# Deferring an elementwise product and respreading matmuls in a Mamba block kernel on eight NeuronCores

## The reference, cut to what matters

```
xn = layernorm(x)                          # x: 16 x 2048 x 1024
xp = xn @ in_proj_w.T + b ; x1, x2 = split(xp)         # 2048 channels each
u  = silu(causal_conv4(x1))
h[t] = dA * h[t-1] + dB * u[t] ; y = sum_n C[n] h[n]   # 16 states per channel
s  = (y * silu(x2)) @ out_proj_w.T + b
hid = silu(xn @ wg.T / 127) * (xn @ wu.T / 127)        # 3072 hidden
g  = silu(hid @ wd.T / 127)
out = x + s * g
```

## Time and profile before

| what | us |
|---|---|
| median of the two runs | 5023.45 (5015.12 and 5031.77) |
| profiled execution, its own time | 4871.78 |
| its span on the slowest core (core 5) | 4870.2 |
| spans of the eight cores | 4815.3 to 4870.2 |
| PE, DVE, ACT busy on core 5 | 3108.9, 2581.7, 1166.5 |

### The profile page before, as it was taken

How to read it: one execution, slowest core, us unless ns; L and a number is a source line. 1 busy time by engine, 2 the same in 40 slices (tenths; PEclk the granted TensorE clock), 3 DMA queues, 4 the chain that set the end, 5 groups by cost and what they waited for, 6 DMA issues and landing times.

```text
span 4870.2 us, 40584 instructions; the slowest of 8 cores (4815.3 to 4870.2 us)
## 1 busy us (share of the span) xinstructions
PE 3108.9 (64%) x14080; PEld 1331.7 (27%) x14080; DVE 2581.7 (53%) x1507; ACT 1166.5 (24%) x1575; POOL 169.4 (3%) x324
## 2 busy tenths in 40 slices
PE   3565666666656478767646666656666654777787
PEld 2222222222222134333322222222222221333333
DVE  2777777877777501000137877777778783010001
ACT  6111111111111023432351111111111111334322
POOL 0000000000000000000000000000000000000000
PEclk9777777777777599999868777777777776999877
DMA  3000100011000334432320010001000003353222
GB/s 93 18 18 16 26 18 18 16 26 18 18 15 18 84 57 104 85 49 52 88 64 18 18 24 18 18 15 26 18 18 20 18 11 99 55 139 48 46 44 61
DMA packets 84574, 196.07 MB, mean 40 GB/s; under 512 B 10272, under 2 KB 27040, under 8 KB 84384
## 3 DMA queue, kind: packets, MB, share of 16 engines
q0 software_dynamic: 46080, 109.07, 14.0%
q1 hardware_dynamic: 38304, 84.40, 5.1%
HBM read 268.93 MB, written 33.55 MB: 62 GB/s over the span
## 4 chain that ended last, share of the span: by engine, by line
PE 39%; DVE 25%; issue 22%; ACT 11%; DMA 2%; SPq 1%; DVEq 0%; ACTq 0%; POOLq 0%
DVE bfb L593 22%; PE ps_a L444 7%; PE ps_b L444 6%; ACT bfa L162 5%; PE ps_a L807 4%; PE ps_b L499 4%; PE ps_b L807 4%; PE ps_y L613 4%; PE ps_a L499 3%; PE ps_a L709 3%; PE ps_b L709 2%; DVE bfb L601 2%; ACT s_sb L457 1%; ACT bfb L162 1%; PE ps_t L155 1%
## 5 line engine op out<-in xcount | busy, mean ns | idle before, releaser
L593 DVE TENSOR_TENSOR_SCAN bfb<-aa,bfb 128x2048 bf16<-128x2048 f32 x512 | 2262.1, 4418 | 155.0 <-PE ps_y L613 107.1
L613 PE MATMUL ps_y<-bfb 128*128 128x512 bf16 x2048 | 745.6, 504 | 1021.0 <-DVE bfb L601 1021.0
L613 PEld LDWEIGHTS ps_y<-bfb 128*128 128x128 bf16 x2048 | 211.5, 114 | 1495.7 <-issue 1412.3
L467 DVE TENSOR_TENSOR bfa<-s_sb 128x1024 bf16<-128x1024 bf16 x96 | 66.5, 692 | 1017.9 <-ACT s_sb L457 1017.9
L444 PE MATMUL ps_a<-xnt,bfa 128*128 128x512 bf16 x1536 | 418.1, 421 | 288.8 <-ACT bfa L162 285.8
L749 DVE TENSOR_TENSOR bfb<-f32a,s_sb 128x1024 bf16<-128x1024 f32 x32 | 39.2, 1225 | 824.0 <-PE ps_t L155 643.6
L162 ACT ACTIVATE bfa<-ps_t 128x1024 bf16<-128x1024 bf16 x320 | 319.4, 1020 | 255.9 <-PE ps_t L155 251.9
L444 PE MATMUL ps_b<-xnt,bfa 128*128 128x512 bf16 x1536 | 377.0, 390 | 0.0
L499 PE MATMUL ps_a<-xnt,bfa 128*128 128x512 bf16 x1024 | 322.3, 472 | 2.6 <-ACT bfb L520 1.4
L499 PE MATMUL ps_b<-xnt,bfa 128*128 128x512 bf16 x1024 | 317.8, 466 | 0.0
L444 PEld LDWEIGHTS ps_a<-xnt,bfa 128*128 128x128 bf16 x1536 | 146.9, 104 | 484.6 <-issue 376.8
(11 more groups left out here) (60 smaller groups left out, 1835.7 us busy)
## 6 DMA issues: line engine op xcount, KB each, us to landing
f32a<-x SPq DMA_DIRECT2D x64, 512.0 KB, 7.6
bfa<-wg POOLq DMA_DIRECT2D x96, 256.0 KB, 3.6
bfa<-wu POOLq DMA_DIRECT2D x96, 256.0 KB, 3.6
bfb<-wd POOLq DMA_DIRECT2D x32, 768.0 KB, 6.7
bfa<-win POOLq DMA_DIRECT2D x64, 256.0 KB, 5.8
xg_spill<-bfb SPq DMA_DIRECT2D x32, 512.0 KB, 2.6
bfa<-wout POOLq DMA_DIRECT2D x32, 512.0 KB, 5.2
bfb<-xg_spill SPq DMA_DIRECT2D x128, 128.0 KB, 6.4
```

The costliest lines, as they stand in the source:

```text
L467: (lambda mh: lambda e: e.tensor_tensor(bfa[:, 8192 + 1024 * mh:8192 + 1024 * (mh + 1)], s_sb[:, 0:1024], s_sb[:, 1024:2048], ALU.mult))(mh),
L593: (lambda i, n, hs, uslot: lambda e: e.tensor_tensor_scan(hs, sb["aa"][:, 16 * i + n:16 * i + n + 1].broadcast_to([128, T]), uslot, 0.0, A ...
L613: (lambda n, pc, dg, hs: lambda e: e.matmul(ps["y"][:, 512 * pc:512 * (pc + 1)], dg, hs[:, 512 * pc:512 * (pc + 1)], start=(n == 0), stop= ...
```

## The change

The product of both halves is no longer appended right after the unit with hi = 1. It is put on a list and appended to DVE's queue at the start of the next `emit_f1` (`flush_hm`). `s_sb` has two slots for the halves, by mh mod 2, and PE's wait before a unit with hi = 0 is for the product of mh - 2. The units inside a block move from n = 4 and 8 to n = 6 and 12, the convolution from n = 9 to n = 13, and the input pieces 4 and 5 from behind the gate product to n = 9 and 11.

```diff
+        pending_hm = []
+
+        def flush_hm():
+            while pending_hm:
+                mh, sl = pending_hm.pop(0)
+                wh = [("ss", ev_mm_evac[(mh, 1, 1)])] + \
+                    ([h_guard[0]] if mh == 0 else [])
+                ev_hm[mh] = op("vector",
+                               (lambda mh, sl: lambda e: e.tensor_tensor(
+                                   bfa[:, 8192 + 1024 * mh:8192 + 1024 * (mh + 1)],
+                                   s_sb[:, 2048 * sl:2048 * sl + 1024],
+                                   s_sb[:, 2048 * sl + 1024:2048 * sl + 2048],
+                                   ALU.mult))(mh, sl),
+                               waits=wh, inc="sv")
+                ev_hm_prev[0] = ev_hm[mh]
 
         def emit_f1(u, cb, count):
             for _ in range(count):
+                flush_hm()
...
                             if p == 0 and hi == 0:
-                                w.append(("sv", ev_hm_prev[0]))
+                                w.append(("sv", ev_hm[mh - 2] if mh >= 2
+                                          else ev_hm_prev[0]))
...
-                    dst = s_sb[:, 1024 * hi + 512 * p:1024 * hi + 512 * (p + 1)]
+                    dst = s_sb[:, 2048 * sl + 1024 * hi + 512 * p:
+                               2048 * sl + 1024 * hi + 512 * (p + 1)]
                     wev = [("st", lastm)]
-                    if g_guard[0] is not None:
+                    if g_guard[0] is not None and mh <= 1:
                         wev.append(g_guard[0])
-                        g_guard[0] = None
...
                 if hi == 1:
-                    wh = [("ss", ev_mm_evac[(mh, 1, 1)])] + \
-                        ([h_guard[0]] if mh == 0 else [])
-                    ev_hm[mh] = op("vector",
...
+                    pending_hm.append((mh, sl))
...
-                if n in (1, 3, 5, 7) and i + 1 < NI:
+                if n % 2 == 1 and n <= 11 and i + 1 < NI:
                     emit_ip_piece(i + 1, n // 2)
-                if n in (4, 8):
+                if n in (6, 12):
                     emit_f1(u, 0, 1)
-                if n == 9 and i + 1 < NI:
+                if n == 13 and i + 1 < NI:
                     emit_conv(i + 1)
...
             if i + 1 < NI:
-                emit_ip_piece(i + 1, 4)
-                emit_ip_piece(i + 1, 5)
                 emit_ip_piece(i + 1, 6)
                 emit_ip_piece(i + 1, 7)
```

More of the change, by code:

```diff
@@ L425, in emit_f1 @@
                 f1_idx[0] += 1
+                sl = mh % 2
                 wnm, act = (("wg", AF.Silu) if hi == 0 else ("wu", AF.Identity))
@@ L461, in emit_f1 @@
                     rot.release(idx, "ss", ev_mm_evac[(mh, hi, p)])
+                if mh == 1 and hi == 1:
+                    g_guard[0] = None
                 ws_f1.consumed(slot, lastm)
                 if hi == 1:
-                    wh = [("ss", ev_mm_evac[(mh, 1, 1)])] + \
-                        ([h_guard[0]] if mh == 0 else [])
-                    ev_hm[mh] = op("vector",
[L467 to L472, removed]
+                    pending_hm.append((mh, sl))
         ip_state = {}
```

## The result

The changed kernel's median is 4358.87 us (11 runs, 4253.44 to 4475.77), that of the kernel before 4921.65 us (10 runs, 4829.57 to 5031.77). The ratio is 0.881, with a 95% interval of 0.8789 to 0.8831. The profiled execution took 4257.52 us, its slowest core (core 5) 4256.0 us, the eight cores 4235.8 to 4256.0.

A forecast was written before the change was run, and what follows sets the result against it. DVE's in-order queue, idle about 339 us per scan stage, was taken to set the stages' period; savings of 280.3 + 279.7 in them and 9 outside, 569 us, gave 4454 us from 5023.5, range 4300 to 4540 (4290 to 4590 with part of (a)).

The forecast's parts named there:

- The product emitted late: Scan stages: emitting the FFN product L467 later in DVE's queue removes its whole wait, 250.3 us in the first stage.
- Units and pieces in the middle of a block, 0: Inside scan-stage blocks: the moved units, pieces and convolution on PE cause no new DVE wait, 0 us.
- The boundary: Between blocks: gates wait 1.42 us (23.6 per stage with one 2.26), third scans mean 2.25 us (31.5 per stage).
- The last block, 2 x 2.06 us: Last block of each scan stage: both units hold the scan behind them up 2.06 us, 4.1 us per stage.
- The FFN stage outside, 9 us: FFN stage outside the scans: with a second slot, first-half units no longer wait for L467, 9 us saved.
- From the profiled execution to the result: Whole kernel: the same 569 us taken off the profiled 4871.8 us gives 4303, off the two-run median 5023.5 gives 4454.
- The rule on 13/16 of the clock: Skill's rule that dense matmuls on three cores lower a die's clock; some 105 us lost, near 4560; left out of the sum.
- (a): Rival: PE's backlog makes units at steps 6 and 12 hold scans up; 9.8 us per block, 4650 us; chance 0.13.
- (b): Rival: the wait on L467 is not what holds DVE; only two moved pieces help, 104 us, 4919; chance 0.02.
- (c): Rival: PE at 1.2 GHz through the whole scan stage, a block 98.8 us against 97.5, slower at 5065; chance 0.03.
- (d): Rival: PE slower at block boundaries, gates 2.26 us, third scans 3.4 late; 57 us less saved, 4511; chance 0.10.

## Why the prediction was right

**The product emitted late**: right. 250.3 us of waits went to none, and the queue kept its work.

**Units and pieces in the middle of a block, 0**: right. In the first fifteen blocks of the stage DVE waits nowhere between the third scan and the gate. The experiment with the convolution at step 12 shows that the limit is real.

**The boundary**: right for the gates, 15 at 1.42 and one at 2.26 worked out as 23.6 us, measured 23.4. For the third scans 31.5 was worked out, 31.7 less the 0.9 below, 30.8, was measured; but the single waits are not the 2.54 and 1.93 that were worked out: one of the fourteen is none at all, ten lie between 1.45 and 2.34, and three are 4.0. The sum took one length for each instruction on PE at every boundary; in the trace the first piece takes 3.56 to 3.58 us before the three long waits and 1.89 before the others but the first (3.48), and the unit's first half anything from 1.87 to 3.44. So the total of the third scans is right in part by luck: shorter and longer waits cancel. (The mean of 2.54 and 1.93 is 2.24, not 2.25; it changes the sum by 0.2 us.)

**The last block, 2 x 2.06 us**: too much. One wait of 0.92 us is there, before scan 9, behind the unit at step 6, and none in the second stage:

```profile
1337.89 4.42 DVE L605 TENSOR_TENSOR_SCAN bfb<-aa,bfb 128x2048 bf16<-128x2048 f32 x1 [0.92 <-PE ps_y L625]
```

The unit before it, first in the changed kernel, then the second half of the one in the earlier trace rows in the kernel before:

```profile
1331.75 3.44 PE L462 MATMUL ps_a<-xnt,bfa 128*128 128x512 bf16 x8 [1.48 <-ACT bfa L162]
1335.03 1.89 PE L462 MATMUL ps_b<-xnt,bfa 128*128 128x512 bf16 x8
```

```profile
1602.42 2.33 PE L444 MATMUL ps_b<-xnt,bfa 128*128 128x512 bf16 x8
```

The second half runs wholly at 2.4 GHz now (1.89 us) and took 2.33 before, and the first half 3.44 instead of 3.57; that is 0.57 us of the 1.14 between the two waits; where the rest lies is not shown. The unit at step 12 made no wait here.

Together 59.2 us of idle time were worked out and 55.1 measured; the stages are 1263.5 and 1261.5 us, 1270 was said.

**The FFN stage outside, 9 us**: wrong. The step was "with the second slot, a first-half unit no longer waits for L467". The mean wait is the same with two slots and with one (1.58 us), and the same as before (1.57), so the guard on the product did not end last there. What makes some of these waits 1.61 to 1.8 us long, no run here looked for.

**From the profiled execution to the result.** On its own terms 4303 was forecast and 4257.5 measured, 45.5 us more saved. The scan stages gave 14 of it (286.4 and 287.6 against 280.3 and 279.7), the missing 9 us go the other way, and some 40 us came from outside the scan stages, where the experiment with one slot and the waits of PE show no effect of the change. Those 40 us are in the profile of before: its slowest core was granted less in the last stages than core 0. Here the last stretch of core 0, then of core 5, in the kernel before:

```profile
4580.00:4817.00 237.00, 176.12 (x1030) 88.29 (x1028) 20.30 (x17) 68.05 (x82) 8.47 (x16) 0.91 0.30 63
```

```profile
4600.00:4870.00 270.00, 212.84 (x1024) 99.09 (x1024) 19.61 (x16) 67.15 (x80) 7.38 (x14) 0.74 0.27 55
```

About the same instructions took PE 212.8 us at 0.74 on core 5 and 176.1 at 0.91 on core 0, 36.7 us more. On core 0 the kernel before took 4817.3 us and the changed one 4235.8: 581.5 us less, 569 were forecast; 579.7 of them are the two scan stages (1549.3 and 1549.6 less 1260.4 and 1258.8), and the time outside them is 1718.4 and 1716.6 us. The 4454 us of the prediction, 95 above the measured median of 4358.87, took over the median of the first two runs, which a larger number of runs moved from 5023 down to 4922; in that the reference was off, not the saving. The two medians now differ by 563 us.

**The rule on 13/16 of the clock** (the Trainium skill, "TensorE: Matmul & The Clock Gate", Part 1) was weighed against one stretch only. In the changed kernel, the same FFN stage has 1.00 again (0.99 to 1.00 on all eight cores), and the scan stage, denser than before, rose to 0.84, so there is no sign of it there:

```profile
1640.00:1890.00 250.00, 179.57 (x1061) 89.24 (x1060) 15.24 (x22) 101.01 (x133) 22.70 (x43) 1.00 0.44 82
```

**The rivals**: (a), (b), (c) and (d) did not come true. (b) falls by the waits before the product, which are gone, (a) by the middle of the blocks, (d) by the gates at 1.42 us. (c) was the furthest: the clock in the scan stage rose instead of staying low. (a) and (d) were near in one respect: the wait of (a) comes with the convolution one product earlier, and the boundary of (d), gates at 2.26 and third scans some 3.4 us late, with the convolution at step 10 (2.25, and 46.1 us over 14 blocks).

## What to carry to other kernels

An in-order engine that bounds a stage should not hold an instruction whose input another engine has yet to make: put it a few steps later, behind work that is ready, and ask by a run whether the second buffer is needed (here it was not). Then ask what the removed wait had been hiding; here 49 us per stage came back at the boundary. Spreading the other engine's burst took that away, and putting ready work of the next block ahead of the dependent gate product took away the gate's own wait. The room inside a block is limited (here about one scan step of 4.48 us): the same 16 matmuls moved ahead of one product cost 109 us.

## What the runs showed of the hardware that was not expected

Moving 16 matmuls three steps earlier, with the same work in all, cost 61 us, most of it since PE entered each boundary at 1.2 instead of 2.4 GHz: the last product took 1.87 instead of 1.02 us, the first piece 3.05 instead of 1.89. Where light work stands on PE is then part of the cost of the heavy work behind it. The level can also differ at places with the same instructions: in one stage of the changed kernel, the first piece behind the gate took 1.89 us at eleven boundaries and 3.48 to 3.58 at four.
